# A four-layer graph kernel: the second layer's identity sums regrouped, and its gathered table stored by vector component

## The reference

```python
# features of a node: 8 scalars (l=0), then 8 vectors (l=1) of 3 components, vector by vector
R = relu(w_e * w1 + b1) @ w2 + b2            # per edge: the radial weights
Y = spherical_harmonics(edge_attr_3)         # per edge, l = 0, 1, 2
msg_blocks = for each output order lo: sum over input order li and filter order lf of
             norm[lo] * einsum('euv,ef,evi,ofi->euo', R[..k], Y[lf], F[src], C[lo,lf,li])
out = segment_sum(msg, dst)
x = layernorm(x + out)
```

## Time and profile before

| | |
|---|---|
| median of 3 runs | 18224.74 us (18221.88 to 18226.33) |
| profiled execution, its own time | 18232.07 us |
| its span, first to last instruction | 18230.3 us |
| TensorE clock granted, mean over the span | 0.753 of full |
| busy: PE / DVE / ACT / POOL | 12464.4 / 10965.0 / 3002.1 / 11528.9 us |
| layer 2's loop | about 6600 to 10823 us of the span |

### The profile page before, as it was taken

The page is one execution under the profiler, slowest core; times in us unless marked ns, Lnnn a source line. Parts: engine busy times, 40 slices in busy tenths (PEclk is TensorE's granted clock), DMA queues, the critical chain, the costliest instruction groups (busy, mean ns, idle before and its releaser), DMA issues. The chain is left out here.

```text
span 18230.3 us, 301015 instructions
## 1 busy us (share of the span) xinstructions
PE 12464.4 (68%) x95607; PEld 6973.8 (38%) x95607; DVE 10965.0 (60%) x19696; ACT 3002.1 (16%) x5708; POOL 11528.9 (63%) x10055
## 2 busy tenths in 40 slices
PE   0466555555555557877878864676666765999999
PEld 0344433433333334544444431222222222455554
DVE  2465554444444459999999985333333335577776
ACT  0122222222222211111111110111111110000000
POOL 4788888888888867777777767777777773000000
PEclk6565555555555579999999986777777667999999
DMA  8233333333333332222222224444444443799998
GB/s 316 46 39 39 38 38 37 38 39 37 38 37 38 38 63 65 64 67 65 65 66 64 66 48 61 91 85 91 92 85 91 91 85 98 232 288 292 301 290 262
DMA packets 3002797, 1816.43 MB, mean 100 GB/s; under 512 B 1734093, under 2 KB 2760210, under 8 KB 2983410
## 3 DMA queue, kind: packets, MB, share of 16 engines
q1 hardware_dynamic: 2206148, 1338.06, 29.1%
q0 software_dynamic: 669312, 166.80, 11.6%
q10 hardware_dynamic: 126512, 300.38, 4.7%
HBM read 1475.61 MB, written 392.90 MB: 102 GB/s over the span
## 5 line engine op out<-in xcount | busy, mean ns | idle before, releaser
L2019 POOL DMA_INDIRECT xg<-d_tab,s_i x3136 | 2973.7, 948 | 1276.7 <-DMA xg<-d_tab,s_i 616.1
L2594 POOL DMA_INDIRECT xg<-d_tab,s_i x3136 | 2993.7, 955 | 957.9 <-issue 903.0
L1403 POOL DMA_INDIRECT d_acc<-AG,ix x1568 | 2467.0, 1573 | 527.2 <-issue 469.0
L1403 POOL DMA_INDIRECT d_acc<-T,ix x1568 | 2464.2, 1572 | 478.0 <-issue 450.3
L2980 PE MATMUL pacc<-nodes,HB 128*32 128x512 fp8e4 x47040 | 2662.8, 380 | 41.1 <-PEq L3024 41.0
L1756 PE MATMUL pm<-ms,eq 128*128 128x32 f32 x6272 | 1363.8, 399 | 888.4 <-PEq L1754 888.3
L2631 DVE TENSOR_TENSOR_SCAN U<-mU,U,up 128x512 f32<-128x512 f32 x392 | 501.6, 1280 | 2365.5 <-DVEq L2630 2364.4
L2980 PEld LDWEIGHTS pacc<-nodes,HB 128*32 128x32 f16 x47040 | 1259.4, 97 | 1317.5 <-issue 56.4
L1756 PEld LDWEIGHTS pm<-ms,eq 128*128 128x128 f32 x6272 | 1341.4, 329 | 932.5 <-issue 931.8
L1035 PE MATMUL pw<-ok,ol 128*128 128x392 bf16 x4048 | 1301.6, 457 | 302.7 <-PEq L1033 302.6
L1023 DVE TENSOR_SCALAR ok<-iotak,kt 128x392 bf16<-128x392 f16 x4048 | 1379.6, 392 | 0.0
(11 more groups left out here) (346 smaller groups left out, 18526.5 us busy)
## 6 DMA issues: line engine op xcount, KB each, us to landing
packed<-d_A SPq DMA_DIRECT2D x420, 1792.0 KB
row<-d_m SPq DMA_DIRECT2D x1568, 64.0 KB
xg<-d_tab,s_i POOLq DMA_INDIRECT x6272
wrow<-d_w SPq DMA_DIRECT2D x392, 256.0 KB
d_scan<-so ACTq DMA_DIRECT2D x392, 256.0 KB
d_A<-stage ACTq DMA_DIRECT2D x97, 784.0 KB
d_ea<-in_ea_t ACTq DMA_DIRECT2D x1, 50176.0 KB, 224.6
d_exp<-T ACTq DMA_DIRECT2D x1, 50176.0 KB, 246.9
```

The lines of the kernel that those rows point to most:

```text
L1403: e.indirect_dma_start(out=d_acc[i], out_offset=bass.IndirectOffsetOnAxis(ap=ix[k][:, t:t + 1], axis=0), in_=mo[k][:, t * F:(t + 1) * F], ...
L2019: e.indirect_dma_start(out=xg[n][:, t, :], out_offset=None, in_=d_tab, in_offset=bass.IndirectOffsetOnAxis(ap=s_i[n][:, t:t + 1], axis=0)) ...
L2594: e.indirect_dma_start(out=xg[n][:, j * ST + c, :], out_offset=None, in_=d_tab, in_offset=bass.IndirectOffsetOnAxis(ap=s_i[d][:, col:col + ...
```

## The change

It touches layer 2 in three places. The identity sums on PE stand in parts of 4, 6, 4 and 2, the last behind radial(7), in place of 6, 5 and 5. On ACT spread goes ahead of early_sums. The table that layer 2 gathers from holds the eight vectors component by component: POOL copies each piece of XN into T1, first the 8 scalars, then the 24 vector features reordered, and SP stores T1; head reads them accordingly.

```diff
--- before.py
+++ after.py
@@ -1792,15 +1792,21 @@
                             e.dma_start(to[:, of, :], d_acc[i][0:NP, :].rearrange("(b p) f -> p b f", p=P)[:, of, :]
                                         ).then_inc(S(f"bk{j}"), 16)
                     for of in SUMS:
+                        e.wait_ge(S("part_t"), 2)
+                        e.sem_inc(S("part_t"), -2)
+                        e.dma_start(tab_v[:, of, :], T1[:, of, :]).then_inc(S("cp"), 16)
+                    e.wait_ge(S("cp"), 16 * len(SUMS))
+                    e.sem_inc(S("cp"), -16 * len(SUMS))
+
+                @block.gpsimd
+                def _(e):
+                    e.memset(wT[:, :], 0.0).then_inc(S("wz"), 1)
+                    for of in SUMS:
                         e.wait_ge(S("tab"), 1)
                         e.sem_inc(S("tab"), -1)
-                        e.dma_start(tab_v[:, of, :], XN[:, of, :]).then_inc(S("cp"), 16)
-                    e.wait_ge(S("cp"), 16 * len(SUMS))
-                    e.sem_inc(S("cp"), -16 * len(SUMS))
-
-                @block.gpsimd
-                def _(e):
-                    e.memset(wT[:, :], 0.0).then_inc(S("wz"), 1)
+                        e.tensor_copy(T1[:, of, 0:8], XN[:, of, 0:8]).then_inc(S("part_t"), 1)
+                        e.tensor_copy(T1[:, of, 8:32].rearrange("p b (i v) -> p b i v", i=3),
+                                      XN[:, of, 8:32].rearrange("p b (v i) -> p b i v", i=3)).then_inc(S("part_t"), 1)
 
                 @block.vector
                 def _(e):
@@ -2074,9 +2080,9 @@
                             e.sem_inc(S("past_" + e.engine.name), 1)
                         e.wait_ge(S(f"eP{n % 2}"), 1)
                         e.sem_inc(S(f"eP{n % 2}"), -1)
-                        of = xg[n][:, :, 8:32].rearrange("p t (v i) -> p t v i", i=3)
+                        of = xg[n][:, :, 8:32].rearrange("p t (i v) -> p t i v", i=3)
                         for i in range(3):
-                            last = e.tensor_tensor(hp[:, i, :, :, :], bc(of[:, :, :, i], 1, 3), bc(eP[n % 2][:, :, :, i], 3, 8),
+                            last = e.tensor_tensor(hp[:, i, :, :, :], bc(of[:, :, i, :], 1, 3), bc(eP[n % 2][:, :, :, i], 3, 8),
                                                    ALU.mult)
                         last.then_inc(S("hd"), 1)
 
@@ -2259,24 +2265,24 @@
                     hidden(0)
                     spread(0)
                     hidden(1)
+                    spread(1)
                     early_sums(0)
-                    spread(1)
                     with e.Fori(0, G // 4 - 1) as it:
                         for n in range(4):
                             scalars(n % 2)
                             frames((n + 2) % 4)
                             hidden((n + 2) % 4)
                             give((n + 2) % 4)
+                            spread((n + 2) % 4)
                             early_sums((n + 1) % 2)
-                            spread((n + 2) % 4)
                             scan_store(e, b, it * 4 + n, n % 2)
                     for n in range(2):
                         scalars(n)
                         frames(n + 2)
                         hidden(n + 2)
                         give(n + 2)
+                        spread(n + 2)
                         early_sums(1 - n)
-                        spread(n + 2)
                         scan_store(e, b, G - 4 + n, n)
                     scalars(0)
                     early_sums(1)
@@ -2375,16 +2381,17 @@
                         radial(n, 2, past)
                         radial(n, 3, past)
                         radial(n, 4, past)
-                        early_sums(0, 6)
+                        early_sums(0, 4)
                         radial(n, 5, past)
                         if past:
                             columns((n + 3) % 4)
-                        early_sums(6, 11)
+                        early_sums(4, 10)
                         radial(n, 6, past)
-                        early_sums(11, 16)
+                        early_sums(10, 14)
                         if not last:
                             turn(0, 3)
                         radial(n, 7, past)
+                        early_sums(14, 16)
 
                     turn(0, 3)
                     step(0, past=0)
```

More of the change, by code:

```diff
@@ L1794, in _ @@
                     for of in SUMS:
-                        e.wait_ge(S("tab"), 1)
-                        e.sem_inc(S("tab"), -1)
-                        e.dma_start(tab_v[:, of, :], XN[:, of, :]).then_inc(S("cp"), 16)
+                        e.wait_ge(S("part_t"), 2)
+                        e.sem_inc(S("part_t"), -2)
+                        e.dma_start(tab_v[:, of, :], T1[:, of, :]).then_inc(S("cp"), 16)
                     e.wait_ge(S("cp"), 16 * len(SUMS))
@@ L1803, in _ @@
                     e.memset(wT[:, :], 0.0).then_inc(S("wz"), 1)
+                    for of in SUMS:
+                        e.wait_ge(S("tab"), 1)
+                        e.sem_inc(S("tab"), -1)
+                        e.tensor_copy(T1[:, of, 0:8], XN[:, of, 0:8]).then_inc(S("part_t"), 1)
+                        e.tensor_copy(T1[:, of, 8:32].rearrange("p b (i v) -> p b i v", i=3),
+                                      XN[:, of, 8:32].rearrange("p b (v i) -> p b i v", i=3)).then_inc(S("part_t"), 1)
                 @block.vector
```

## The result

The changed kernel takes 18282.18 us (median of 8 runs, 18273.45 to 18289.66) against 18228.28 us of the kernel before (8 runs beside it): a ratio of 1.003, 95% interval 1.002 to 1.0039. It is slower by 54 us, though VectorE has less to do in each step and TensorE the same, in another order.

A forecast was written before the change was run, and what follows sets the result against it. VectorE was taken to bound layer 2's steps, TensorE at u = 7, with slow clock hits. The clock takes the gain back: +31 us, table 0.6, +32 on 18232.1 gives 18264, less 7.3 for the median, 18256; range 18120 to 18296.

The forecast's parts named there:

- the third rival: Layer 2 loop: two steps of three hit by the slow clock, 21.66 us a step, +65 us, 18290 us; chance 0.23.
- The sums, 0.66 us earlier: TensorE, layer 2: 14 sums instead of 16 ahead of radial(7), starting it 0.66 us earlier; VectorE's 0.21 us wait goes.
- The products of head(), 91 ns each: VectorE's head(): three products fall from 645 to 554 ns with contiguous sources, 0.27 us a step.
- The second rival: VectorE's head(): products stay at 645 ns, step 20.53 us, -39 to -110 us, mid 18150 us; chance 0.10.
- The undisturbed step, 20.26 us: Layer 2 step without a slow clock stretch: 20.74 - 0.21 - 0.27 = 20.26 us on VectorE.
- A long hit 2.7, a short one 1.5 us: Time a step loses to a half-clock stretch: 2.7 us (2.2 to 3.2) for 6.83 us, 1.5 for 3.42.
- ACT's order, POOL's copies of the table: ScalarE: spread() before the pQ copies, price 0; POOL: the last table piece's copies and handover, 0.6 us once.
- The clock: TensorE's granted clock in layer 2: shorter steps lose the old beat, more are hit, the gain goes; chance 0.45.
- steps between 21.31 and 21.66, mid 21.49: Mean layer 2 step with one long and one short hit in four or three steps: 196 x (21.49 - 21.33) = +31 us.
- The first rival: Layer 2 loop: hits stay rare, one long in four -77 us, 18148 us; none -210 us, 18015 us; chance 0.18.
- POOL's gathers: POOL, layer 2: 948 ns each plus about 0.3 us of issue, 16 x 1.25 = 20.0 us a step, not yet late.
- 196 x (21.33 - 20.26) = 210 us gained: Layer 2 loop, 196 steps: the gain from the shorter step if the clock were always full, 210 us.

## Why the prediction was wrong or right

The predicted time, 18256 us, was 26 us low; the result lies inside the range and on the slower side, which had the highest chance. Of the 26 us 3.5 lie in the kernel before, whose median came as 18228.28 in place of 18224.74: +32 us was forecast, +54 came. What came was the third rival, two steps of three hit, with a chance of 0.23: it named 21.66 us a step and 18290 us, and 21.62 and 18282 were measured. The same 21.66 is the upper end of the forecast's own span. The loop's clock was 0.92, where 0.93 was named.

- *The sums, 0.66 us earlier, and the wait of 0.21 us ahead of products(7) gone*: right, 1.10 us there, and right that they end within the gap behind radial(7).
- *The products of head(), 91 ns each*: right, 100 ns measured (645 to 545). The second rival falls. The trace thereby decides between the two operands: the step of three floats in SBUF was the whole excess, and the operand in PSUM that stayed as it was costs VectorE nothing visible. That is a weak test of a step in PSUM, since each of its values is read eight times in a row; the line L2093 of the earlier trace rows is the better one. The Trainium skill, "Advanced Engine Details and Errata", section "SBUF Cachelines", says that reads which do not meet the same 16 bytes twice lose speed; the run with the table alone agrees, its product takes 541 ns. The rule of section "PSUM Cachelines", which is about matmuls, carried over to VectorE would have given 0, and 100 ns were measured.
- *The undisturbed step, 20.26 us*: 20.19 measured, 0.03 of the difference from the products and 0.03 from the pair at products(7) (1.10 us, where 1.13 was taken). *A long hit 2.7, a short one 1.5 us*: 22.94 - 20.19 = 2.75 and 21.72 - 20.19 = 1.53.
- *ACT's order, POOL's copies of the table*: right. The last two copies took 0.196 and 0.243 us.
- *The clock*: the mechanism was right, and shown: filled pauses bring the clock to 0.99 and take 162 us off the changed kernel (172 with each set against the kernel before of its own rounds). The term that was mis-sized is "steps between 21.31 and 21.66, mid 21.49". I took the middle between a pair of stretches in four steps and a pair in three, though nothing in the trace spoke for a mixture, and the earlier trace rows showed a beat that was fixed over 17 repetitions. The changed kernel kept one pair in three steps nearly through the whole loop. The mid between the two cases brought the number nearer to the result than the case with one pair in four steps would have, and that was luck. The runs with 50 elements more or with the ring show that mixtures do exist (two pairs in seven or eight steps), so only the traces settle which it is.
- *The first rival, hits stay rare because TensorE is busier on average*: not for this kernel, but it is what the sums alone did. The Trainium skill, "TensorE: Matmul & The Clock Gate", Part 1, lets the gate follow how busy TensorE has been recently. Read as an average over steps it fails: between slow stretches the changed kernel has TensorE busy for 83% of the time (31.06 of 37.54 us, in the windows above), the sums alone for 81% (327.97 of 406.18), and that kernel has the rarer slow stretches. Read of the pauses themselves it agrees with the idle matmuls.
- *POOL's gathers, "16 x 1.25 = 20.0 us a step: next in line, not yet late"*: right for this kernel, but undersized. With the ring of four and the pauses filled they take 20.8 us, since landings are waited for too. At an always full clock the sum "196 x (21.33 - 20.26) = 210 us gained" could not have come: with the idle matmuls and the ring of four it was 18237.6 - 18119.8 = 118 us, with the ring of eight 204.

## What to carry to other kernels

Where the granted clock falls in a fixed beat, look for the pauses ahead of the stretches and fill them before tuning anything else: two idle matmuls in each of two pauses gave 126 us to the old kernel and 162 to the changed one, while less work alone cost 54. Why these pauses bring a beat of three steps or of four was not found, so the trace has to be read again after each edit. Judge a change to such a loop at full clock, since a tenth of a microsecond can move the beat either way. And count for a queue of transfers not only its issues but what each waits to land, here 0.45 us a step beyond the usual gap.

## What was not expected of the hardware

The same pair of slow stretches, a long one of 6.83 us and a short one of 3.42 us 23.9 us later, occurs in six kernels (changed, 50 and 200 elements more, ring of eight, sums alone, sums with the ring), from once in three steps to 11 times in 196. And the time is not monotonic in VectorE's work: 0.24 us more a step, 47 us in all if nothing else moved, took the ratio from 1.003 to 0.9954.
